# The expert stage and output phase of a graph, attention and mixture-of-experts kernel: eight output blocks in flight in place of four, three result buffers in place of two, and a group's result turned one step sooner

## What is computed

```python
x = x + relu(A_norm @ (layernorm(x) @ W.T))        # graph convolution, adj is 8192 x 8192
z = layernorm(x)                                   # attention over all rows, causal, 4 heads
z = z + attention(rmsnorm(z)) @ wo.T
flat = rmsnorm(z)
weights = top2(softmax(flat @ router_w.T))         # normalised over the two
for e in range(8):
    hh = silu(flat @ w1[e].T) * (flat @ w3[e].T)   # 341 hidden units
    out = out + weights[:, e:e + 1] * (hh @ w2[e].T)
x = x + z + out
```

## Time and profile before

| | us |
|---|---|
| median of 3 runs | 3520.46 (3517.39 to 3522.1) |
| the profiled execution, its own time | 3524.27 |
| its span, first to last instruction | 3522.5 |
| TensorE busy | 3085.2 (88%) |
| VectorE busy | 2554.2 (73%) |
| first `up` matmul of the expert loop starts | 3188.97 |
| last `up` matmul starts | 3453.19 |
| last scatter of the drain starts | 3471.12 |
| first load of the output phase is issued | 3473.25 |

### The profile page before, as it was taken

The page is one execution under the profiler, slowest core; times in us unless marked ns, Lnnn a source line. Parts: engine busy times, 40 slices in busy tenths (PEclk is TensorE's granted clock), DMA queues, the critical chain, the costliest instruction groups (busy, mean ns, idle before and its releaser), DMA issues. The chain is left out here.

```text
span 3522.5 us, 56503 instructions
## 1 busy us (share of the span) xinstructions
PE 3085.2 (88%) x22241; PEld 1353.5 (38%) x22241; DVE 2554.2 (73%) x2736; ACT 1423.8 (40%) x2843; POOL 1728.2 (49%) x1113
## 2 busy tenths in 40 slices
PE   2678889899989987998999999999999999957992
PEld 1334434344434432433433333333333333324661
DVE  8888887675554455779878977877987898616773
ACT  0000000000000003666666666666666666745661
POOL 0000000000321113776888699877699869763665
PEclk9778999999999997999999999999999999988996
DMA  9898876678667944440000000000000000002224
GB/s 376 349 391 366 349 308 267 282 296 302 254 261 292 359 155 167 160 164 13 29 18 18 7 24 17 11 8 7 7 17 18 11 2 17 9 26 93 74 74 154
DMA packets 157501, 506.75 MB, mean 144 GB/s; under 512 B 20081, under 2 KB 66298, under 8 KB 112326
## 3 DMA queue, kind: packets, MB, share of 16 engines
q1 hardware_dynamic: 111400, 448.58, 32.9%
q10 hardware_dynamic: 33024, 31.47, 2.7%
q0 software_dynamic: 12816, 23.11, 2.0%
HBM read 426.31 MB, written 75.37 MB: 142 GB/s over the span
## 5 line engine op out<-in xcount | busy, mean ns | idle before, releaser
L1223 DVE TENSOR_REDUCE unit_max<-ps_max 128x2 f32<-128x1024 f32 (+2 forms) x1088 | 1225.9, 1171 | 297.4 <-PE ps_max L1452 254.1
L998 POOL TENSOR_TENSOR chunk_sum<-chunk_sum,probs 128x1024 f32<-128x1024 f32 x480 | 1132.3, 2359 | 287.8 <-ACT probs L1093 277.1
L1093 ACT ACTIVATE probs<-ps_ring 128x512 f32<-128x512 f32 x2112 | 1089.8, 596 | 440.2 <-PE ps_ring L1471 408.1
L566 PE MATMUL ps_gather<-ring,keep_attended 128*128 128x512 f32 x1688 | 789.8, 625 | 140.1 <-DMA ring<-in_adj 121.4
L1471 PE MATMUL ps_ring<-q_stack,keep_shared 97*128 97x512 f16 x2112 | 673.9, 385 | 27.7 <-ACT probs L1093 22.2
L1486 PE MATMUL ps_acc<-probs,keep_shared 128*32 128x256 f32 (+1 forms) x8448 | 566.8, 386 | 0.0
L566 PEld LDWEIGHTS ps_gather<-ring,keep_attended 128*128 128x128 f32 x1688 | 332.6, 202 | 541.7 <-issue 541.7
L367 DVE TENSOR_TENSOR work<-work,ring 128x2048 f32<-128x2048 f32 x195 | 446.6, 2290 | 34.5 <-DMA ring<-in_adj 30.7
L342 POOL DMA_DIRECT2D scratch_lower<-lower x13 | 7.3, 560 | 805.0 <-ACT lower L484 805.0
L1452 PE MATMUL ps_max<-k_heads,q_heads 32*128 32x512 f16 (+3 forms) x2176 | 276.0, 378 | 69.9 <-DVE unit_max L1223 48.5
L1495 PE MATMUL ps_acc<-probs,keep_ones_heads 128*32 128x256 f32 (+1 forms) x4224 | 327.9, 380 | 0.0
(11 more groups left out here) (243 smaller groups left out, 2667.5 us busy)
## 6 DMA issues: line engine op xcount, KB each, us to landing
ring<-in_adj SPq DMA_DIRECT2D x302, 1024.0 KB, 13.9
keep_shared<-in_adj SPq DMA_DIRECT2D x45, 1024.0 KB, 10.8
scratch_slots<-empty_rows SPq DMA_DIRECT2D x16, 2080.0 KB, 14.3
moe_x_rows<-scratch_slots SPq DMA_DIRECT2D x39, 260.0 KB, 2.7
moe_parts<-scratch_parts SPq DMA_DIRECT2D x32, 256.0 KB, 4.2
x_in<-in_x SPq DMA_DIRECT2D x16, 256.0 KB, 13.3
x_in<-in_x ACTq DMA_DIRECT2D x16, 256.0 KB, 7.5
work<-in_cos ACTq DMA_DIRECT2D x16, 256.0 KB, 4.1
```

Source lines behind the costliest of these rows:

```text
L566: last = nc.tensor.matmul(bank[:], support[:, s * SUB + c, :], tile_of[g, is_again][:, c * BT:(c + 1) * BT], start=(first and c == 0), sto ...
L998: steps.then(nc.gpsimd.tensor_tensor(totals, totals, weights, ALU.add))
L1093: nc.scalar.activation(probs[:, q % SLOTS, i, kv, :, lo:], halves(bank)[:, :, lo:], ACT.Exp, scale=SCALE).then_inc(ring_read, 1)
L1223: nc.vector.tensor_reduce(unit_max[:, half % 2, heads, s % 2, unit], ps_max[:, base:base + HEADS, at:at + width], AX_X, ALU.max).then_inc( ...
```

## The change

The output phase gets eight buffers `parts` in place of four, `y_rows` and `y_index` get three in place of two, TensorE turns a group's result in step f = 0 in place of f = 1, and VectorE scales it in f = 1 in place of f = 2.

```diff
-    BUFFERS = 2
-    PB = 4
+    BUFFERS = 3
+    PB = 8
...
-        y_rows = sb("y_rows", [P, 2, SUB, C])
-        y_index = sb("y_index", [P, 2, SUB], mybir.dt.uint32)
+        y_rows = sb("y_rows", [P, BUFFERS, SUB, C])
+        y_index = sb("y_index", [P, BUFFERS, SUB], mybir.dt.uint32)
...
             def scale_parts(g):
                 dve.wait_ge(x_loaded[g % XB], 16 * (g // XB + 1))
-                if g >= 2:
+                if g >= BUFFERS:
                     dve.wait_ge(y_scattered[g % BUFFERS], 16 * SUB * (g // BUFFERS))
-                nc.vector.tensor_copy(y_index[:, g % 2, :], x_rows[:, g % XB, :, C + 1])
+                nc.vector.tensor_copy(y_index[:, g % BUFFERS, :], x_rows[:, g % XB, :, C + 1])
                 dve.wait_ge(y_turned, g + 1)
-                nc.vector.tensor_tensor(y_rows[:, g % 2], split(ps_y[:]),
+                nc.vector.tensor_tensor(y_rows[:, g % BUFFERS], split(ps_y[:]),
                                         x_rows[:, g % XB, :, C:C + 1].to_broadcast([P, SUB, C]), ALU.mult
                                         ).then_inc(y_scaled, 1)
...
-                if f == 2 and g >= 2:
+                if f == 1 and g >= 2:
                     scale_parts(g - 2)
...
-                if f == 1 and g >= 2:
+                if f == 0 and g >= 2:
                     turn_moe(g - 2)
```

## The result

The changed kernel takes 3610.4 us (median of 4 runs, 3605.6 to 3615.3) where the kernel before takes 3521.3 (4 runs): ratio 1.0254, 95% interval 1.0236 to 1.0272. It is 89 us slower; the forecast was 3609. The profiled execution took 3615.3 us, its span is 3613.6.

The account below looks back on a forecast made before the run. The prediction took TensorE to bound the expert loop, with every wait paid in full. Loop 93.6 us slower, drain 1 and output 4 faster, gave 88.6 us more: 3609 us, 2.5% slower, range 3590 to 3626.

Parts of the forecast that it names:

- TensorE is the bound and every wait is paid in full: Expert loop: TensorE busy for 241.00 of 241.00 us, so each wait it gets there lengthens the loop in full.
- The turn waits 1.45 us for the copy: TensorE, f = 0: result transposes wait for ScalarE's copy, starting 2.08 us after T, the last `up` matmul's start; 1.45 taken.
- `x_lo` has no slack: VectorE, f = 1: scaling ahead of `x_lo` starts the next group 3.92 us behind the last `up` matmul, not 3.25.
- Period 9.31: Expert loop: one group takes 9.31 us in place of 6.75, which is 2.56 more.
- The loop's term: Expert loop: 36 groups pay 2.56 us each and group 38 pays 1.45 alone, together 93.6 us slower.
- The drain: After the loop: scatters follow without a gap thanks to the third buffer; last one 16.8 us behind last `up`; gain 1 us.
- The output phase: Final loads and stores: eight blocks in flight cut idle time only; gain between 0 and 6.5 us, 4 taken.
- DMAs queued sooner do not shorten the 40.5 us of packets: Output phase: the engines' 40.5 us of packet time stays; only the 6.5 us of idle time can shrink.
- SyncE's waits for stores: Output phase: SyncE's 24.4 us of waits for stores before it can load would be almost gone with eight blocks.
- Only the turn costs: Rival, loop: `x_lo` is not held by VectorE's order; a group pays 1.45 us at the low end, 3569 us; chance 0.07.
- no wait arises: Rival, loop: the copy finishes early enough, TensorE goes through, only drain and output count; 3515 us; chance 0.03.
- The clock falls: Rival, loop: idle gaps lower TensorE's clock; 3637 us at mean 0.90, 3692 at 0.75; chance 0.09 for 3630 and up.

Follow-up runs that it names:

- stores held apart: Kernel before with sixteen blocks in flight and ScalarE's queue issuing its first store only once all blocks are added: 3519.5 us in one run.
- both orders mended: Changed kernel with ScalarE's copy ahead of its gate and `x_lo` ahead of VectorE's scaling: 3527.7 us against 3522.3 for the kernel before, ratio 1.0015.

## Why the prediction was right

- **TensorE is the bound and every wait is paid in full.** Shown: the two waits add up to 86.5 us as drawn in the changed kernel, and its loop is 94.7 us longer; with the copy moved the one wait goes, and the loop shortens by 54.3. The drawn waits are the smaller, as the prediction said.
- **The turn waits 1.45 us for the copy.** Shown by the timeline (transposes at T + 2.07, forecast T + 2.08) and by moving the copy alone, which gave back 54.3 us, forecast 54.
- **`x_lo` has no slack, and the scaling ahead of it costs 0.67 us.** Shown by the scaling alone, 23.5 us for 36 groups, 0.65 each, and by the turn alone, where `x_lo` held TensorE from its old place.
- **Period 9.31.** Measured 9.33. The loop's term was 93.6 and came out at 94.7: the first matmuls behind each of the two waits stand a few hundredths further apart (0.49 us from the `ps_y` transposes to the next matmul, 0.46 in the sum).
- **The drain.** GpSimd started on group 36 at 1.83 us behind the last `up` matmul, forecast 1.84, and scattered without a gap; 1.5 gained, 1 forecast, since the 1.36 a scatter included two odd long ones. The prediction's reason for the scatters without a gap, the third buffer, is not it: with two buffers and both moves the drain is 16.4 us just the same.
- **The output phase is the term that was mis-sized:** 4 us, range 0 to 6.5, measured 9.6. The step that failed is "DMAs queued sooner do not shorten the 40.5 us of packets". They did: the stores' DMA time stayed at 14, but the loads' fell from 26.5 to 23.1. That is 3.5 of the 9.6 us; the other 6.1 are time in which the engines are not counted busy, where 4 was forecast (in the stretches shown it fell from 6.5 to 1). Profiles with four blocks give 25.9 to 26.7 for the loads and outputs of 49.3 to 51.7 us; with eight, 22.9 to 23.3 and 39.4 to 40.4; with sixteen, 22.8 to 23.3 and, with the stores not held, 36.9 to 37.3. The packets in the traces show where the 3.5 us sit. More than nine in ten of the 4096 load packets of 2 KB take 84 ns or close to it, before and after. Before, 219 take over 150 ns, after only 87; what these take beyond 84 ns is 4.5 and 1.2 us of DMA time. After, nearly all of it (1.1) falls in the first 10 us of the loads. Before, 3.4 of the 4.5 fall within 4 us of a point where SyncE issues loads again behind a pause of over 2 us. The changed kernel has three such points too, and no long packet there. What makes these packets slow is not settled. It is not the mixing with stores (held apart, nothing is saved), nor simply the depth (two blocks cost less DMA time than four).
- **SyncE's waits for stores** were to be taken away by eight blocks, and were halved (24.4 to 12.9 us). With sixteen they are gone, and the output phase is only 2 us shorter still, so with eight the 12.9 us cost 2 us at most.
- The total came out at the forecast in part by luck: the output term was 5.6 us too small a gain, so the stages give 83.7 us. The medians stand 89.1 apart, against 88.6 forecast; the 5.4 us between stages and medians are not in the changed code (the two profiles began their loops 7.4 us apart).
- **The rivals.** "Only the turn costs" is out by the scaling alone; "no wait arises" by the timeline. "The clock falls" is out: the granted clock is 1.00, the level of 2.4 GHz, over 330 us in which TensorE idles twice in every 9.33 us, 1.25 and 0.94 us as drawn. The rule of the Trainium skill ("TensorE: Matmul & The Clock Gate", A second HAM failure mode), that frequent short idles make the clock oscillate, does not show here; the measurement decides.
- The Trainium skill's 425 GB/s ("DMA: Bandwidth & Descriptors", Bandwidth) would by the prediction's estimate have made the output phase 17 us shorter; the loads alone came to 403 in their middle and the stores to 336, and the phase lost 9.6. Of the reasons that the prediction gave against it, the mixing of reads and writes is out, by the stores held apart.

The best kernels here are those with eight or sixteen blocks in flight and the old order of turn and scaling, 3508.8 to 3513.4 us, 0.2 to 0.4% below the kernel before.

## What to carry to other kernels

Before an operation is moved forward in the order of the engine that is the bound, measure the distance between the end of what it needs and its start: here 0.58 us of slack against a move of 1.95 us. Look as well at what the operation covered where it stood; the turn's 0.43 us of matmuls stood exactly over a chain on another engine, and with both orders mended the sooner turn still cost 15 us. When a queue of transfers is not kept full, its packets' busy time is no floor, since that time itself can shrink when more are in flight, and the waits of the engine that issues them are no measure of a loss either: 12.9 us of them cost at most some 2 us here.

## What was not expected of the hardware

The DMA time of the same 8.39 MB of loads depends on how the transfers are spaced: 25.3 us with two blocks in flight, 25.9 to 26.7 with four, 22.8 to 23.3 with eight or sixteen, while that of the stores stays at 13.9 to 14.1. The difference sits in a few per cent of the packets, as told above. In the profile of the changed kernel the 16 DMA engines move 12.59 MB in 38 us, 331 GB/s, against 268 over the 47 us before.
